# A layer-norm step moved from ScalarE to VectorE in a one-core attention and feed-forward kernel on Trainium2

## What is computed

```python
def _layernorm(x, axis=-1, eps=1e-05):
    m = jnp.mean(x, axis=axis, keepdims=True)
    v = jnp.var(x, axis=axis, keepdims=True)
    return (x - m) / jnp.sqrt(v + eps)

# 16 heads of 8 channels, length 256; k = v = context, q = layernorm(x)
kv  = jnp.einsum('bhil,bhjl->bijhl', k_, v_)
y   = causal_convolution(kv, ssm_kernel) + kv * D
x   = x + jnp.einsum('bijhl,bhil->bjhl', y, q_)
# feed-forward: 256 -> 704 -> 256, integer weights with a scale per row
h   = layernorm(x)
x   = x + (silu(h @ Wg.T) * (h @ Wu.T)) @ Wd.T
```

## Time and profile before

| | us |
|---|---|
| median of 3 runs | 76.23 |
| lowest and highest run | 76.20 and 77.52 |
| span of the profiled execution, first to last instruction | 74.5 |
| busy on TensorE, VectorE, GpSimd, ScalarE within the span | 69.8, 61.7, 58.8, 45.5 |

### The profile page before, as it was taken

One profiled execution on the slowest core, in us unless ns is written; L12 is line 12 of the kernel. 1 busy time (PEld: TensorE's weight loads), 2 busy tenths in 40 slices (PEclk: granted clock), 3 DMA queues, 4 the chain that ended last, 5 costly groups with the idle time before them and its releaser, 6 DMA issues.

```text
span 74.5 us, 1494 instructions
## 1 busy us (share of the span) xinstructions
PE 69.8 (94%) x470; PEld 57.7 (77%) x470; DVE 61.7 (83%) x187; ACT 45.5 (61%) x115; POOL 58.8 (79%) x76
## 2 busy tenths in 40 slices
PE   5999989999999989999999999999999999999920
PEld 4666557988878848889798889797999989899810
DVE  0078899999988999999999899999968884586760
ACT  1503436464867879967746894657768796776400
POOL 6033587997999999899999999479998999339230
PEclk9999999999999999999999999999999999999998
DMA  0898999999997000000000000000002006000404
GB/s 8 235 254 230 372 315 364 324 382 392 361 356 224 29 0 0 0 0 4 9 0 0 0 0 4 0 0 0 0 13 70 0 0 210 1 9 0 140 1 141
DMA packets 7128, 8.29 MB, mean 111 GB/s; under 512 B 816, under 2 KB 6224, under 8 KB 7120
## 3 DMA queue, kind: packets, MB, share of 16 engines
q1 hardware_dynamic: 6768, 7.88, 33.0%
q10 hardware_dynamic: 352, 0.31, 1.2%
HBM read 7.12 MB, written 1.07 MB: 110 GB/s over the span
## 4 chain that ended last, share of the span: by engine, by line
PE 68%; POOL 16%; DVE 9%; issue 2%; ACT 1%; POOLq 0%; DVEq 0%
PE conv L1018 26%; PE down L1037 13%; POOL products L387 10%; PE conv L985 6%; PE turn L1058 5%; PE conv L994 5%; PE conv L996 5%; POOL rstd_q L371 4%; PE turn L965 3%; DVE terms L731 3%; PE turn L947 2%; PE turn L1037 2%; POOL terms L279 2%; DVE terms L734 1%; DVE terms L738 1%
## 5 line engine op out<-in xcount | busy, mean ns | idle before, releaser
L1018 PE MATMUL conv<-f_parts,wgu 128*128 128x256 f16 x176 | 22.1, 273 | 0.0
L387 POOL TENSOR_TENSOR products<-k_skip 128x512 f32<-128x512 f32 (+1 forms) x16 | 18.2, 1147 | 1.2 <-DMA k_skip<-ctx_skip 1.2
L1018 PEld LDWEIGHTS conv<-f_parts,wgu 128*128 128x128 f16 x176 | 16.6, 98 | 2.7 <-DVE hidden L746 0.2
L257 POOL TENSOR_TENSOR h_lo<-hidden,h_hi 128x256 fp32r<-128x256 f32 x18 | 13.1, 745 | 2.6 <-ACT h_hi L527 2.5
L746 DVE SCALAR_TENSOR_TENSOR hidden<-conv,su_sb,gate_act 128x256 f32<-128x256 f32 (+1 forms) x24 | 11.5, 482 | 3.0 <-ACT gate_act L522 2.8
L522 ACT ACTIVATE gate_act<-conv,sg_sb 128x256 f32<-128x256 f32 (+1 forms) x24 | 11.2, 467 | 4.2 <-PE conv L1018 3.9
L985 PE MATMUL conv<-products,toeplitz 128*128 128x288 f32 x32 | 11.3, 437 | 0.1
L731 DVE TENSOR_TENSOR terms<-conv,q_ext 128x512 f32<-128x512 f32 x16 | 10.9, 682 | 0.5 <-ACT q_ext L504 0.3
L994 PE MATMUL conv<-products,toeplitz 128*128 128x288 f32 x32 | 10.6, 413 | 0.3 <-DVE toeplitz L664 0.3
L996 PE MATMUL conv<-products,toeplitz 128*128 128x288 f32 x32 | 10.4, 406 | 0.0
L527 ACT ACTIVATE h_hi<-hidden 128x256 fp32r<-128x256 f32 x20 | 8.3, 413 | 3.4 <-DVE hidden L746 3.1
(11 more groups left out here) (64 smaller groups left out, 121.6 us busy)
## 6 DMA issues: line engine op xcount, KB each, us to landing
k_skip<-ctx_skip SPq DMA_DIRECT2D x3, 384.0 KB, 5.9
toeplitz<-taps_pad SPq DMA_DIRECT2D x2, 512.0 KB, 8.6
out<-x_sb SPq DMA_DIRECT2D x7, 128.0 KB, 1.7
toeplitz<-matrices SPq DMA_DIRECT2D x3, 256.0 KB, 5.4
wg_int<-wg_t SPq DMA_DIRECT2D x1, 704.0 KB, 7.6
wu_int<-wu_t SPq DMA_DIRECT2D x1, 704.0 KB, 8.8
wd_int<-wd_t SPq DMA_DIRECT2D x1, 640.0 KB, 10.0
x_sb<-x SPq DMA_DIRECT2D x1, 512.0 KB, 5.1
```

The costliest lines, as they stand in the source:

```text
L257: eng.tensor_tensor(low_of(i, t), hidden[up_lanes(t), i % 2, t, :], high_of(i, t), ALU.subtract).then_inc(done, 1)
L387: nc.gpsimd.tensor_tensor(view(products[:, n:n + 1], first * MADE + GROUP, [[MADE, halves], [GROUP, 4], [1, GROUP]]), view(k, 0, [[EXT * B ...
L1018: done = nc.tensor.matmul(bank_of(i, t)[:, n, :], wgu[:, c, column:column + P], f_parts[:, i % 2, part, c, :], start=(c == 0 and part == 0 ...
```

## The change

VectorE's `norm_q` and `norm_f` take the place of `shift_of_q` and `shift_of_f`, at the same sixteen places in VectorE's list. Each now reads the whole tile of `x_sb` and writes the normed rows in one `tensor_scalar`, with mean and rstd as per-row scalars. ScalarE's sixteen `norm_q` and `norm_f` and the tensors and semaphores of the shift go; the rest of ScalarE's list keeps its order. Each new instruction has a second wait, for the transposition that read the same row buffer two tiles earlier.

```diff
-            def norm_q(t):
-                wait(act, q_shift, t + 1)
-                nc.scalar.activation(q_rows[:, t % 2, :], x_sb[:, t, :], ACT.Identity, bias=shift_q[:, t:t + 1],
-                                     scale=rstd_q[:, t:t + 1]).then_inc(q_normed, 1)
-
-            def norm_f(t):
-                wait(act, f_shift, t + 1)
-                nc.scalar.activation(f_rows[:, t % 2, :], x_sb[:, t, :], ACT.Identity, bias=shift_f[:, t:t + 1],
-                                     scale=rstd_f[:, t:t + 1]).then_inc(f_normed, 1)
...
-            norm_q(0)
             evict_q(0)
             act.wait_ge(k_loaded[2], 16)
             squares(2)
             squares(3)
-            norm_q(1)
             wrap(0)
...
-            def shift_of_q(t):
+            def norm_q(t):
                 wait(dve, q_rstd, t + 1)
-                dve.tensor_scalar(shift_q[:, t:t + 1], moments_q[:, t, 0:1], rstd_q[:, t:t + 1], -1.0,
-                                  ALU.mult, ALU.mult).then_inc(q_shift, 1)
+                wait(dve, q_turned, t - 1)
+                dve.tensor_scalar(q_rows[:, t % 2, :], x_sb[:, t, :], moments_q[:, t, 0:1],
+                                  rstd_q[:, t:t + 1], ALU.subtract, ALU.mult).then_inc(q_normed, 1)
...
-            def shift_of_f(t):
+            def norm_f(t):
                 wait(dve, f_rstd, t + 1)
-                dve.tensor_scalar(shift_f[:, t:t + 1], moments_f[:, t, 0:1], rstd_f[:, t:t + 1], -1.0,
-                                  ALU.mult, ALU.mult).then_inc(f_shift, 1)
+                wait(dve, f_turned, t - 1)
+                dve.tensor_scalar(f_rows[:, t % 2, :], x_sb[:, t, :], moments_f[:, t, 0:1],
+                                  rstd_f[:, t:t + 1], ALU.subtract, ALU.mult).then_inc(f_normed, 1)
...
             moments_of_f(0)
-            shift_of_q(3)
+            norm_q(3)
             multiply_terms(4)
...
             add_sum(1)
-            shift_of_f(0)
+            norm_f(0)
             stats_of_q(5)
...
             merge_back(dve, 2)
-            shift_of_q(4)
+            norm_q(4)
             moments_of_q(6)
...
```

More of the change, by code:

```diff
@@ L101, in build @@
         rstd_q = sb("rstd_q", [P, TILES])
-        shift_q = sb("shift_q", [P, TILES])
         stats_f = sb("stats_f", [P, TILES, 6])
@@ L106, in build @@
         rstd_f = sb("rstd_f", [P, TILES])
-        shift_f = sb("shift_f", [P, TILES])
         wg_int = sb("wg_int", [P, HALVES, HID], I32)
@@ L153, in build @@
         q_rstd = sem("q_rstd")
-        q_shift = sem("q_shift")
         q_normed = sem("q_normed")
@@ L169, in build @@
         f_rstd = sem("f_rstd")
-        f_shift = sem("f_shift")
         f_normed = sem("f_normed")
@@ L559, in _ @@
             squares(4)
-            norm_q(2)
             squares(5)
@@ L568, in _ @@
             convert_gate()
-            norm_q(3)
             wrap(2)
@@ L572, in _ @@
             evict_q(3)
-            norm_f(0)
-            norm_q(4)
             convert_up()
@@ L578, in _ @@
             evict_q(4)
-            norm_f(1)
             squares(11)
@@ L582, in _ @@
             high_f(1)
-            norm_q(5)
             convert_down()
@@ L590, in _ @@
             hidden_high(0, 0)
-            norm_q(6)
             hidden_high(0, 1)
@@ L601, in _ @@
             gate(0, 3)
-            norm_f(2)
             gate(0, 4)
             high_f(2)
-            norm_f(3)
             high_f(3)
@@ L608, in _ @@
             wrap(5)
-            norm_q(7)
             gate(0, 5)
@@ L614, in _ @@
             hidden_high(0, 4)
-            norm_f(4)
             high_f(4)
@@ L623, in _ @@
             wrap(7)
-            norm_f(5)
             hidden_high(1, 2)
@@ L636, in _ @@
             gate(2, 2)
-            norm_f(6)
             hidden_high(2, 2)
@@ L640, in _ @@
             high_f(6)
-            norm_f(7)
             gate(2, 4)
@@ L773, in _ @@
             variance_of_q(0)
-            shift_of_q(0)
+            norm_q(0)
             dve.wait_ge(k_loaded[1], 16)
@@ L789, in _ @@
             stats_of_q(2)
-            shift_of_q(1)
+            norm_q(1)
             moments_of_q(2)
@@ L797, in _ @@
             direct(5)
-            shift_of_q(2)
+            norm_q(2)
             moments_of_q(3)
@@ L830, in _ @@
             stats_of_q(7)
-            shift_of_f(1)
+            norm_f(1)
             moments_of_q(7)
@@ L836, in _ @@
             low_f(0)
-            shift_of_q(5)
+            norm_q(5)
             variance_of_q(6)
@@ L847, in _ @@
             hidden_units(0, 0)
-            shift_of_q(6)
+            norm_q(6)
             hidden_units(0, 1)
@@ L855, in _ @@
             moments_of_f(3)
-            shift_of_f(2)
+            norm_f(2)
             variance_of_f(3)
@@ L863, in _ @@
             stats_of_f(4)
-            shift_of_f(3)
+            norm_f(3)
             hidden_units(0, 4)
@@ L869, in _ @@
             moments_of_f(4)
-            shift_of_q(7)
+            norm_q(7)
             variance_of_f(4)
@@ L873, in _ @@
             merge_last(dve, 5)
-            shift_of_f(4)
+            norm_f(4)
             hidden_units(0, 5)
@@ L888, in _ @@
             scale_out(0, 0)
-            shift_of_f(5)
+            norm_f(5)
             hidden_units(1, 3)
@@ L904, in _ @@
             moments_of_f(7)
-            shift_of_f(6)
+            norm_f(6)
             variance_of_f(7)
@@ L908, in _ @@
             hidden_units(2, 2)
-            shift_of_f(7)
+            norm_f(7)
             scale_out(1, 0)
```

## The result

The changed kernel takes 85.94 us (85.77 to 87.22, four runs) beside 76.27 for the kernel before in the same series: a ratio of 1.125, interval 1.1205 to 1.1296. The forecast was 81.5 with a range up to 84.0. The direction and the place were right, the loss of 9.7 us was near twice the 5.3 that I gave. The first profile of the changed kernel fell in a slow run at a lower clock; the lines here are of a second series of it (86.54 us, 1.130, span 84.5 us, 10.0 more than before).

What follows compares the result with a forecast made beforehand. The prediction took VectorE and TensorE, both full from 10 to 51.6 us, as the bound. Longer instructions (1.8 us) plus holds (4.7), less absorption, gave 5.3 us: a span of 79.8, with 1.7 around it 81.5 us, range 76.8 to 84.0.

Steps and rivals of the forecast that it cites:

- VectorE and TensorE both full, ScalarE's relief worth nothing: From 10 to 51.6 us neither engine runs ahead; ScalarE's 9.6 us less work was costed at nothing.
- The hold: Thirteen row writes in the full stretch wait for wide GpSimd instructions: 0.36 us each, 4.7 us, ends 0 and 8.5.
- The length: Thirteen row writes in the full stretch step 0.26 us, 0.14 more than a shift: 1.8 us, ends 0 and 3.5.
- the sum: Over the span: 1.8 us longer instructions plus 4.7 us of holds, less what is absorbed, gives 5.3 us.
- its third rival: Worse: late VectorE merges and matrix fixes also meet GpSimd's wide instructions; eight merges add 2.9 us, 84.4; chance 0.08.
- One is cheap: The first row write, at 5.95 us, lies ahead of the full stretch and was counted as cheap.
- the two behind the stretch: The f rows of tiles 6 and 7, after 51.6 us, where VectorE has 1.8 us of room, counted as cheap.
- what is absorbed: VectorE's idle 0.88 us in the full stretch and about 0.3 us that TensorE can wait swallow part of the cost.
- No hold: Rival: in the full stretch VectorE pays only for the longer instruction; 76.8 to 78.5 us, chance 0.27.
- Not slower: Rival: rows come sooner, TensorE's gaps at 27.15 and before the hidden units swallow the cost; 75.7 to 76.5, chance 0.13.

Runs made afterwards that it cites:

- the reduction's kernel: Changed kernel with the sixteen row writes as a tensor_reduce over one element, a plain copy without mean and rstd: 79.62 us, 1.042.
- each accumulating one: Changed kernel with the sixteen row writes as tensor_scalar that also writes a sum over the row, rstd left out: 82.56 us, 1.078.
- the pair with narrow GpSimd work: GpSimd's products of heads 4 to 15 left out, its merges cut to one column: changed kernel 78.99 us, kernel before 75.67.
- the gap filled: Changed kernel with thirty unused matmuls in TensorE's list, ahead of the sum of tile 2: 86.06 us, 1.1274.
- Without the products: Changed kernel without GpSimd's wide products of heads 4 to 15, TensorE using head 3's instead: 82.78 us, 1.0848.

## Why the prediction was wrong in size

*VectorE and TensorE both full, ScalarE's relief worth nothing.* Right. VectorE's idle time in the full stretch is unchanged (0.84 us beside 0.88), and ScalarE's 8.2 us bought nothing that shows.

*The hold.* Right, and sized 0.65 us too low. I took a row write to meet a wide instruction with a share of 0.56 and to wait 0.64 us if it does, 4.7 us for thirteen. Seven of the thirteen are held. Less the 0.40 of an unheld one they wait 0.34 (q row 1), 0.97 (q 2), 1.06 (f 0), 0.35 (q 5), 0.57 (q 6), 0.96 (f 4) and 1.10 (f 5): 5.35 us, 0.76 each. The other six take 0.37 to 0.43. For all sixteen it is 5.75, with f row 7's 0.4; the difference to the reduction's kernel gave 5.9.

*The length.* An unheld row write steps VectorE on by some 0.29 to 0.33 us (19.44 to 19.73 for one), where I took 0.26. Less the shift's 0.12 that is 0.20 each, 2.6 us in place of 1.8. By the Trainium skill, "VectorE: DVE Perf Modes", section "The perf-mode tier table", `tensor_scalar` on fp32 in SBUF works at 2x and `tensor_reduce` at 1x. At 256 elements the runs show no such difference: the unheld plain write takes 0.37 to 0.43, the reduction of the same size 0.42 in the mean. The step of 0.20 that I estimated from the table does not come out; the measured 0.3 decides.

*The step that failed is the sum*: it added row writes and holds and left everything else on VectorE as it was. The prediction had the missing term in hand, as its third rival: VectorE's own two-tensor instructions held by GpSimd, 2.9 us at a chance of 0.08. They cost 2.5. That was no alternative to the hold of the rows, both happen in one kernel. The argument against it, that merges start when GpSimd is done, was true of the old order alone: in the kernel before, VectorE's merges and fixes start where GpSimd rests, ends or comes second. Four places lose that. At three of them, the fix at 18.79 (0.63 long), the merges at 25.48 and 34.26 (1.13 and 0.91), VectorE arrives late beside a wide GpSimd instruction, and at 63.12 a merge (1.28) starts with a low part. The first place, 6 to 8.3 us, is another matter: its 1.0 us of the 2.5 needs early data as well, as shown above. The Trainium skill ("SBUF — State Buffer", section "Who interferes with whom") states both rules side by side, that a VectorE instruction with two SBUF inputs contends with a GpSimd instruction that reads SBUF, and that plain tensor_scalar does in its two-port modes, its accumulating form not. The runs agree on all three: 1.13 for a merge of 0.68, 1.46 for a row write of 0.40, 0.53 for each accumulating one. I had drawn on it for the row writes alone.

*"One is cheap"*, and the two behind the stretch. Wrong as it stands: 1.4 us by themselves. For the first row it held where the data came late (4.31 against 4.46 us) and failed where they came early. Of the 1.0 us between 6 and 8.3 us the half on the products comes from the 0.2 us of its length, which let GpSimd start first; the half on the fix came with early data and the shift as well (0.82). F row 7 is held for 0.4, and TensorE waits those 0.4.

The sum anew: 2.6 for length, 5.35 for holds, 2.5 for two-tensor instructions, 1.0 for the three outer rows (0.2, 0.2 and 0.6) make 11.45, where the span grew by 10.0. How late VectorE is at one and the same instruction shows where the rest of 1.45 went:

```profile
58.55 1.50 DVE L684 TENSOR_SCALAR f_rows<-x_sb,moments_f,rstd_f 128x256 f32<-128x256 f32 x1
59.97 0.47 DVE L718 SCALAR_TENSOR_TENSOR hidden<-conv,su_sb,gate_act 128x256 f32<-128x256 f32 x1
```

The hidden units behind f row 5 started at 50.89 before, so VectorE is 9.1 us late there, and the end comes 10.0 late. Ahead of this place 10.05 us of the sum stand for 9.1, behind it 1.4 (the merge at 63.12, f rows 6 and 7) for 0.9. My 1.2 for what is absorbed was near. But VectorE's old idle time went into it and a new wait of 0.57 for ScalarE, at 31.59, took its place, so that the idle time in the full stretch looks unchanged. Against the forecast of 5.3 the 10.0 are 0.8 more for length, 0.65 for holds, 2.5 and 1.0 for what I had at nothing, less 0.25 for what is absorbed in all.

*The rivals.* No hold at all would have been at most 76.3 plus 3.3, 79.6 by the pair with narrow GpSimd work, in which two rows are still held by 0.75 us together; the 76.8 to 78.5 that I gave it end near there, with the longer instruction under-priced. Not slower falls: it asked for a step under 0.21. The clock I had not weighed; with the gap filled and the clock at 1.00 the time stays as it was. Not settled is how far single places depend on hundredths of a microsecond: the order at one place decides the hold (q row 5 took 0.75 in one trace and 1.42 in the filled one), and what the early data are worth in the median of the runs.

## What to carry to other kernels

Before an elementwise pass goes to VectorE, look at what GpSimd has under way at each of its places: here a plain tensor_scalar from SBUF to SBUF stood still for the rest of the GpSimd instruction (0.40 became up to 1.50), and being late by tenths brought VectorE's own two-tensor instructions into the same wait. Count both in one sum, and ask at each place whether the landing of a DMA decides which engine comes first. If the pass must go there, a form that is not held, even one that takes 0.53 in place of 0.40 us, can cost less; and where two engines are both full, an idle third one is the right place for work that it does slower.

## What the runs showed that I had not expected

GpSimd seems to let go before the end of its record. The merge of 23.00 ends at 24.27 in the record; the row write held by it ends at 24.43, and less its own 0.38 it will have begun at 24.05, 0.22 earlier. Without the products it is the same: 20.52 plus 1.27 is 21.79, 20.69 plus 1.26 less 0.38 is 21.57. This takes it that a released write still needs its own 0.38. Nor does the start in the record say who came first: the row write at 22.97 is recorded 0.03 us ahead of the merge at 23.00 and waits for all of it. The product in front of that merge is recorded until 23.04, so the write may have met that one first.

A row write that comes just too late for one gap waits for the whole next instruction, so the loss goes up in steps; the fill that removed 0.6 us of waiting and got back 0.67 of hold at the next row (1.42 for 0.75) is the plainest case.
